# Key reads of a fused perceiver block shared by two DMA queues, input in four loads, narrow tiles copied by ScalarE

## What is computed

```python
x = x + xattn(layernorm(x), ctx, ctx, Wq, bq, Wk, bk, Wv, bv)   # softmax over 1601 keys
x = x + attn(layernorm(x), ...)     # sigmoid((align-0.295)*15) * gate_q * gate_k, 16 heads of 32
h = layernorm(x)
logits = h @ gate_w.T               # 8 experts
sel, rw = argmax(logits), sigmoid(max(logits))
for e in range(8):
    xs = h * (rw * (sel == e))[:, None]
    out += (xs @ w_up[e].T) * silu(xs @ w_gate[e].T) @ w_down[e].T
x = x + out
```

## Time and profile before

| | us |
|---|---|
| runs | 333.71 median (331.84 to 335.01, 3 runs) |
| the profiled execution | 333.99, its span 332.3 |
| TensorE busy | 301.6 (91%) |
| VectorE busy | 161.2 (49%) |
| ScalarE busy | 90.7 (27%) |
| GpSimd busy | 78.4 (24%) |

### The profile page before, as it was taken

How to read it: one execution, slowest core, us unless ns; L and a number is a source line. 1 busy time by engine, 2 the same in 40 slices (tenths; PEclk the granted TensorE clock), 3 DMA queues, 4 the chain that set the end, 5 groups by cost and what they waited for, 6 DMA issues and landing times. The chain is left out here.

```text
span 332.3 us, 5209 instructions
## 1 busy us (share of the span) xinstructions
PE 301.6 (91%) x1806; PEld 159.8 (48%) x1806; DVE 161.2 (49%) x364; ACT 90.7 (27%) x209; POOL 78.4 (24%) x84
## 2 busy tenths in 40 slices
PE   0999899999899889999989999999998989899792
PEld 0788567643454544445455445455543344443330
DVE  3303338537263763828185833738561354735431
ACT  1132230235112346321234442124411013411110
POOL 5000003167022500112340020135102246103202
PEclk9999999999999999999999999999999999999998
DMA  7999999999999998999949699952715996153300
GB/s 250 390 374 172 184 311 387 211 187 257 387 211 228 279 187 132 375 250 227 324 77 192 116 393 220 258 204 83 298 63 145 396 411 266 28 205 109 119 2 34
DMA packets 61364, 74.27 MB, mean 224 GB/s; under 512 B 3187, under 2 KB 40083, under 8 KB 60320
## 3 DMA queue, kind: packets, MB, share of 16 engines
q1 hardware_dynamic: 59792, 69.23, 80.2%
q0 software_dynamic: 1552, 4.78, 4.0%
HBM read 70.85 MB, written 3.67 MB: 224 GB/s over the span
## 5 line engine op out<-in xcount | busy, mean ns | idle before, releaser
L1251 PE MATMUL SC<-CT_sb,QC_sb 128*64 128x256 f32 x384 | 50.4, 389 | 0.3 <-DVE CT_sb L847 0.2
L847 DVE STREAM_TRANSPOSE CT_sb<-FF_sb 128x1024 f32<-128x1024 f32 x36 | 42.4, 1220 | 14.3 <-DMA FF_sb<-ctx 12.7
L1290 PE MATMUL ST<-CTX_sb,PR_sb 128*64 128x512 f32 (+1 forms) x208 | 48.2, 600 | 1.1 <-ACT PR_sb L347 1.1
L1251 PEld LDWEIGHTS SC<-CT_sb,QC_sb 128*64 128x64 f32 x384 | 24.7, 136 | 17.2 <-issue 9.0
L1176 PE MATMUL A<-AW_sb,normT_sb 128*128 128x512 f32 x64 | 29.4, 599 | 1.3 <-DVE normT_sb L918 1.3
L1290 PEld LDWEIGHTS ST<-CTX_sb,PR_sb 128*64 128x64 f32 (+1 forms) x208 | 13.9, 136 | 23.2 <-issue 22.3
L532 POOL TENSOR_TENSOR rn_sb<-ss_sb,nhalf_sb 128x16 f32<-128x16 f32 x4 | 11.7, 2915 | 33.9 <-DVE ss_sb L923 33.9
L1176 PEld LDWEIGHTS A<-AW_sb,normT_sb 128*128 128x128 f32 x64 | 11.7, 190 | 14.8 <-issue 12.2
L1169 PE MATMUL TR<-ident_sb,CTX_sb 128*128 128x128 f32 (+1 forms) x128 | 16.1, 266 | 2.3 <-DVE CT_sb L340 1.1
L1196 PE MATMUL A<-AW_sb,WQK_sb 128*128 128x256 f32 x64 | 16.4, 422 | 0.8 <-ACT AW_sb L645 0.8
L1169 PEld LDWEIGHTS TR<-ident_sb,CTX_sb 128*128 128x128 f32 (+1 forms) x128 | 12.9, 141 | 8.7 <-issue 5.6
(11 more groups left out here) (227 smaller groups left out, 459.0 us busy)
## 6 DMA issues: line engine op xcount, KB each, us to landing
CTX_sb<-ctx SPq DMA_DIRECT2D x24, 1024.0 KB, 10.7
FF_sb<-ctx SPq DMA_DIRECT2D x80, 128.0 KB, 7.2
FF_sb<-ctx SPq DMA_DIRECT2D x32, 256.0 KB, 7.9
CTX_sb<-wgu SPq DMA_DIRECT2D x4, 1024.0 KB, 9.4
CTX_sb<-wdn SPq DMA_DIRECT2D x5, 512.0 KB, 12.8
FF_sb<-wgu SPq DMA_DIRECT2D x2, 1024.0 KB, 6.6
rows<-XR_sb SPq DMA_DIRECT2D x3, 512.0 KB, 10.7
CTX_sb<-ctx SPq DMA_DIRECT2D x8, 130.0 KB
```

The source lines that it names most:

```text
L847: v.transpose(ctxT[:, pos % 2, k, :, :].rearrange("p c (b r) -> p b c r", r=Q), split[:, k, at:at + BLOCKS, :].rearrange("p b (c r) -> p b ...
L1251: last = t_.matmul(out[q, :], (qcurP if split_group else qcur)[:, c, q], ctxT[:, pos % 2, k, c, 0:n], start=(c == 0), stop=(c == DC - 1))
L1290: last = t_.matmul(ST[q, :], probs[0:w, t, q], ctxb[0:w, k, t, :], start=(t == 0), stop=(t == KT - 1))
```

## The change

SP now issues only the reads of quarters 0 and 1 (`LOWER`, partitions 0 to 63); ScalarE issues those of quarters 2 and 3 (`UPPER`, 64 to 127). Groups 4 and 5 become one part of 256 KB reads. For pair 0 ScalarE's reads stand one by one behind its copies of the queries; later they stand in fours (`upper_first`, `upper_rest`). x is loaded in four pieces with a power each, and the loads of `rowv` and `gwT` are issued behind these powers. TensorE does 9 matmuls on the identity while it waits (`START_FILL`). On VectorE, in pair 0, the transpose of group 1 moves behind the last gate sums and the last copy of numerators. ScalarE copies both narrow tiles, and VectorE reads the number of rounds earlier.

```diff
-SPLIT_PARTS = ((1, 2), (3,), (4,), (5,))
+SPLIT_PARTS = ((1, 2), (3,), (4, 5))
+LOWER, UPPER = ([(quad, k) for quad in range(lo, lo + QUADS // 2) for k in range(2)] for lo in (0, QUADS // 2))
+UPPER_REST, UPPER_FIRST = 1, 5
+START_FILL = 9
-XT_BY_ACT = (3, 5)
+XT_BY_ACT = (3, 4, 5)
...
+        def load_split(eng, p, part, quads):
+            first, slot = SPLIT_PARTS[part][0] * GT * P, SLOT_OF[SPLIT_PARTS[part][0]]
+            n = len(SPLIT_PARTS[part]) * BLOCKS
+            for quad, k in quads:
+                src = A["ctx"][bass.ds(2 * p + k, 1), first:first + n * Q, quad * P:(quad + 1) * P]
+                eng.dma_start(split[quad * Q:(quad + 1) * Q, k, slot * BLOCKS:slot * BLOCKS + n, :],
+                              src.rearrange("a (b r) d -> r (a b) d", r=Q)).then_inc(s_split[part], 16)
...
                 sp.wait_ge(s["keysT_made"], split_turned(p, len(order_of(p).split)))
                 settle(sp)
-                load_split(p + 1, 0)
+                load_split(sp, p + 1, 0, LOWER)
...
                 sp.wait_ge(s["keysT_made"], split_turned(p, 2))
                 settle(sp)
-                load_split(p, 2)
-                load_split(p, 3)
+                load_split(sp, p, 2, LOWER)
...
+            for t in range(PAIRS):
+                if t == 2:
+                    load_weight(wq, "wq", "wq_in")
+                sp.dma_start(xall[:, t, :], A["x"][t * P:(t + 1) * P, :]).then_inc(s[f"x_in{t}"], 16)
...
+            for t in range(PAIRS):
+                pool.wait_ge(s["ln0_eps"], t + 1)
+                g.tensor_tensor(rstd[:, t:t + 1], rstd[:, t:t + 1], nhalf[:, 0:1], ALU.pow).then_inc(s["ln0_pow"], 1)
             pool.dma_start(rowv[:], A["rowv"].partition_broadcast(P)).then_inc(s["rowv_in"], 16)
...
+                    if half == 1:
+                        load_split(act, 0, 0, UPPER[m:m + 1])
...
             for m in range(DC):
                 move_qk(True, m)
+                load_split(act, 0, 1, UPPER[m:m + 1])
...
+            def upper_first(p, n, part):
+                act.wait_ge(s["keysT_made"], split_turned(p, n))
+                if not isinstance(p, int):
+                    settle(act)
+                load_split(act, p + 1, part, UPPER)
+
+            def upper_rest(p):
+                act.wait_ge(s["keysT_made"], split_turned(p, 2))
+                settle(act)
+                load_split(act, p, 2, UPPER)
...
             for t in FIRST.tiles[GT:]:
                 move_keys(act, a.copy, 0, 0, t)
+            upper_first(0, 2, 0)
...
                 move_numerators(act, a.copy, 0, c)
+                if c == 0:
+                    upper_first(0, 3, 1)
...
                     move_keys(act, a.copy, p, 0, NEXT.tile(u))
+                    if u == UPPER_REST:
+                        upper_rest(p)
+                    if u == UPPER_FIRST and not is_last(p):
+                        upper_first(p, NEXT.split.index(3) + 1, 1)
                 exponentials(p)
                 for step in by_max:
                     attention(p - 1, step)
                 move_numerators(act, a.copy, p, 0)
+                if not is_last(p):
+                    upper_first(p, len(NEXT.split), 0)
...
             with act.Fori(0, nr) as r:
-                routed(NT - 1, "xT", r)
+                for f in range(NW, NT):
+                    routed(f, "xT", r)
...
             gate_sums(2, 6)
+            move_numerators(dve, v.tensor_copy, 0, 3)
+            gate_sums(6, 2 * DC)
             turn_split(1, NEXT.groups[0])
-            gate_sums(6, 2 * DC)
-            move_numerators(dve, v.tensor_copy, 0, 3)
             turn_split(1, NEXT.groups[1])
...
-                routed(NW, "xT", link, r)
...
+            for _ in range(START_FILL):
+                t_.matmul(AB[0][:, 0:P], ident[:], ident[:], start=True, stop=True)
```

More of the change, by code:

```diff
@@ L359, in load_ctx @@
                     sp.dma_start(ctxb[0:TAIL, k, FULL, :], src).then_inc(s_ctx[k][c], 16)
-            def load_split(p, part):
-                first, slot = SPLIT_PARTS[part][0] * GT * P, SLOT_OF[SPLIT_PARTS[part][0]]
-                n = len(SPLIT_PARTS[part]) * BLOCKS
-                for quad in range(QUADS):
-                    for k in range(2):
-                        src = A["ctx"][bass.ds(2 * p + k, 1), first:first + n * Q, quad * P:(quad + 1) * P]
-                        sp.dma_start(split[quad * Q:(quad + 1) * Q, k, slot * BLOCKS:slot * BLOCKS + n, :],
-                                     src.rearrange("a (b r) d -> r (a b) d", r=Q)).then_inc(s_split[part], 16)
             def next_split(p):
@@ L421, in _ @@
             sp.sem_inc(s["xr_free"], 16)
-            for i in range(2):
-                src = A["x"][2 * i * P:(2 * i + 2) * P, :].rearrange("(a p) d -> p a d", p=P)
-                sp.dma_start(xall[:, 2 * i:2 * i + 2, :], src).then_inc(s[f"x_in{i}"], 16)
-            load_weight(wq, "wq", "wq_in")
+            for t in range(PAIRS):
+                if t == 2:
+                    load_weight(wq, "wq", "wq_in")
+                sp.dma_start(xall[:, t, :], A["x"][t * P:(t + 1) * P, :]).then_inc(s[f"x_in{t}"], 16)
             load_weight(wkT, "wkT", "wkT_in")
@@ L429, in _ @@
                 load_chunk(0, c)
-            load_split(0, 0)
-            load_split(0, 1)
+            load_split(sp, 0, 0, LOWER)
+            load_split(sp, 0, 1, LOWER)
             sp.wait_ge(s["qp_made"], 2 * DC)
@@ L498, in _ @@
                    allow_small_or_imprecise_dtypes=True).then_inc(s["const_made"], 1)
+            for t in range(PAIRS):
+                pool.wait_ge(s["ln0_eps"], t + 1)
+                g.tensor_tensor(rstd[:, t:t + 1], rstd[:, t:t + 1], nhalf[:, 0:1], ALU.pow).then_inc(s["ln0_pow"], 1)
             pool.dma_start(rowv[:], A["rowv"].partition_broadcast(P)).then_inc(s["rowv_in"], 16)
             pool.dma_start(gwT[:], A["gwT"]).then_inc(s["gwT_in"], 16)
-            for i in range(2):
-                pool.wait_ge(s["ln0_eps"], i + 1)
-                g.tensor_tensor(rstd[:, 2 * i:2 * i + 2], rstd[:, 2 * i:2 * i + 2], nhalf[:, 0:2], ALU.pow).then_inc(s["ln0_pow"], 1)
             def pair_queries(p):
@@ L828, in _ @@
             for i in range(2):
-                dve.wait_ge(s[f"x_in{i}"], 16)
                 for t in range(2 * i, 2 * i + 2):
+                    dve.wait_ge(s[f"x_in{t}"], 16)
                     link(v.bn_stats(st[:, t, :], xall[:, t, :]))
                     link(v.bn_aggr(mv[:, t, :], st[:, t, :]))
-                v.tensor_scalar(rstd[:, 2 * i:2 * i + 2], mv[:, 2 * i:2 * i + 2, 1], EPS, None, ALU.add).then_inc(s["ln0_eps"], 1)
-                dve.wait_ge(s["ln0_pow"], i + 1)
+                    v.tensor_scalar(rstd[:, t:t + 1], mv[:, t, 1:2], EPS, None, ALU.add).then_inc(s["ln0_eps"], 1)
                 for t in range(2 * i, 2 * i + 2):
+                    dve.wait_ge(s["ln0_pow"], t + 1)
                     v.tensor_scalar(xn[:, t, :], xall[:, t, :], mv[:, t, 0:1], rstd[:, t:t + 1], ALU.subtract, ALU.mult).then_inc(s["xn_made"], 1)
@@ L1132, in _ @@
             assert n[0] == COUNT_LINKS
-            for f, step in LATE:
-                routed(f, step, link_wide)
+            routed(*LATE[0], link_wide)
             dve.wait_ge(s["rounds_made"], 1)
             nr = dve.value_load(rounds[0:1, 0:1], min_val=1, max_val=MAXR)
+            for f, step in LATE[1:]:
+                routed(f, step, link_wide)
             with dve.Fori(0, nr) as r:
                 link, n = linker("round_chain", COUNT_LINKS + ROUND_LINKS * r)
-                routed(NW, "xT", link, r)
                 link(v.tensor_scalar(tok[:, 0, :], tok[:, 2, :], 0.0, 2.0 * B * S, ALU.is_equal, ALU.mult))
@@ L1451, in routed @@
                     pe.wait_ge(s_got[f], 16 * r + 16)
-                    earlier(pe, "xT_moved", n)
+                    earlier(pe, "xT_moved", n - 1 if f == NT - 1 else n)
                     turn_rows(x_bank(f), got[f], P).then_inc(s["x_turned"], 1)
```

8 lines of the change are left out of this document (4 added, 4 removed).

## The result

The changed kernel takes 347.32 us (344.1 to 350.17), the kernel before 332.92 beside it: a ratio of 1.0393 with an interval of 1.0301 to 1.0485. It is slower by about 4%; forecast were 335.4 and at most 341. Some executions of most kernels here, the one before included, fall into a slower state, so the ratios, and the times of the experiments if nothing else is said, are those of the other runs (in turn_no_start this leaves out two of twelve, of 449 and 775 us) and can differ a little from the quotient of two medians. The profiled execution took 350.17, its span 348.4; the spans of the five other executions are 342.4 to 347.8, so 0.6 to 6 us of the loss that the profile shows are this execution's own.

The account below looks back on a forecast made before the run. TensorE, busy 301.6 of 332.3 us, was the bound, leaving only its start, waits and half-clock matmuls to shorten. 333.99 with -2.4 - 1.5 - 2.0 + 2.1 + 5.2 = +1.4 gave 335.4; own range 332.7 to 338.8, overall 329.5 to 341.

Parts of the forecast that it names:

- Start: Before the first projections: early matmuls raise TensorE's clock sooner, gaining 2.4 us (3.0 at best), which passes through whole.
- End: Narrow tiles: ScalarE copies the first transpose earlier, so the first narrow matmul starts 1.5 us sooner (0.7 if ScalarE pays VectorE's delay).
- Reads in pair 1: Pair 1: fewer SP issues remove TensorE's waits of 0.95 and 1.14 us, gaining 2.0; pairs 2 and 3 gain nothing.
- Rival 4: Group 4 waits for the whole 2 MB part, about 1 us in each of three pairs; 338.9 us, chance 0.10.
- Pair 0 to 1: End of pair 0: gate sums and transposes behind the last copy make ScalarE's scaling and "on" 2.1 us late; bounds 0 to 2.3.
- Boundaries: Pairs 1 to 2 and 2 to 3: part 0's late upper quarters delay "on" 2.6 us each, 5.2 lost; bounds 3.2 to 7.2.
- Rival 2: ScalarE is held at its read issues, 341 us, chance 0.20; sign: issues over 1.2 us and late copies behind them.
- Rivals 1 and 3: Late upper read of part 0 is covered, 330.2 us (chance 0.28); nine matmuls raise the clock too late, 338.0 (0.06).

Follow-up runs that it names:

- turn_no_start: sync_in_turn with the start of the kernel before (two loads of x, powers of two columns, no early matmuls); ratio 0.9943.
- part2_by_sync: The changed kernel, but SyncE issues all eight reads of part 2 (groups 4 and 5) ahead of the chunk reads; 336.9 us, ratio 1.0111.
- chunks_behind: The changed kernel, but SyncE holds its chunk reads behind part 2 until group 4 has been transposed; 338.55 us, ratio 1.0103.
- start_end_order: The kernel before with the change's start, end and VectorE order at the end of pair 0, all reads as before; ratio 1.0003.
- fill_only: The kernel before with the nine early matmuls alone; ratio 0.9997.
- end_only: The kernel before with the change's end alone (ScalarE copies both narrow tiles, first turns ahead of the loop); ratio 0.9943.
- turn_apart: sync_in_turn with groups 4 and 5 as parts of their own again; 330.68 us, ratio 0.9905.
- sync_in_turn: The changed kernel, but SyncE issues all of part 2 and of pairs 2 and 3's part 0, lower and upper quarters alternating; 329.57 us, ratio 0.9905.
- all_by_sync: The changed kernel with every read back on SyncE, parts still merged; 341.26 us, ratio 1.0240.
- parts_apart: The changed kernel with groups 4 and 5 read as two parts again, both still shared by the two queues; 340.57 us, ratio 1.0166.

## Why the prediction was wrong

- **Start, -2.4.** It was -3.26, a little beyond the good end of its bounds, and the clock was up at 8. "It passes through whole, as TensorE has little idle time behind it up to pair 1" came true for this kernel's reads, though not for the reason it gives, which is luck. With the shared first reads the start did pass: group 3 of pair 1 starts at 91.8 in part2_by_sync and chunks_behind and at 93.69 before, which is the start's 2.6 to 2.7 less the 0.7 that B is longer. In the profiled execution of the change 3.1 of it went to the fall of the clock at 52. With the old reads next to nothing of it passed (start_end_order, fill_only), because part 0 of pair 1 came no earlier, or hardly (transposed at 77.16 and 75.14, at 75.66 before); VectorE already waited 1.86 us for it in the kernel before, and the forecast had not looked there.
- **End, -1.5.** Right: -1.53, and -1.41 in end_only.
- **Reads in pair 1, -2.0, "in pairs 2 and 3 nothing".** This step failed, and it is the largest error. Half of the -2.0 came: the wait of 0.95 us for chunk 0 is gone. For the other half and the "nothing" stand +2.93, +3.37 and +2.30 (C, E, G), 9.6 of the 14.7 us by which the span missed the forecast. The reading of the 1.14 us was right, as it is 0.22 in turn_apart, where group 4 is there in time, but its condition "if groups 4 and 5 land in time" did not hold. The forecast asked how many issues SyncE saves, and not what stands beside ScalarE's reads once they are in a queue of their own. In SyncE's one queue part 2 went ahead of the chunks. In two queues, the half that was issued late shared the engines with chunks that were wanted last.
- **Rival 4** had the place (group 4) but not the cause: it priced the merged part at 180 GB/s as 1 us a pair. The merged part alone costs nothing in pair 2 and up to 0.8 in pair 3, and in pair 1 between nothing (part2_by_sync, turn_no_start) and 3 to 4 (sync_in_turn against turn_apart, all_by_sync against start_end_order); what decides that, no run here shows. In pairs 2 and 3 of the change it took the competing queue as well to make it 3.4 and 2.3.
- **Pair 0 to 1, +2.1.** Right, at 1.9: the reduction ahead of the scaling (L894, now L924) starts 5.97 us behind TensorE's last turn of pair 0, and started 4.09 behind it. B as a whole, with the reads' gain in it, is +0.7 (42.58) where the clock stays up and part 0 is there.
- **Boundaries, +5.2.** The mechanism and the wait were right: part 0 was there 9.1 and 7.4 us behind ScalarE's copy, forecast were 8 to 9, and "on" came 3.2 and 2.5 us later, 5.7 in all. Where the clock stayed up (F of part2_by_sync, parts_apart and chunks_behind) the boundary cost 2.5 to 2.8, the forecast's 2.6. The term missed the clock behind a stop: D and F of the change lost 8.5, the rest of it behind the two falls of the clock.
- **Rival 2** is refuted as a cost, though its sign is there once: four issues took ScalarE 1.9 to 3.7 us, one of them alone 2.07, and behind the slowest four an activation (L710) came 0.8 us late (4.89 us idle ahead of it for 4.06 in pair 3), for which TensorE did not wait:

```profile
162.28 3.73 ACTq L359 DMA_DIRECT2D FF_sb<-ctx  x4
166.12 0.69 ACT L710 ACTIVATE vs_sb<-A,ratio_sb 128x512 f32<-128x512 f32 x1 [4.89 <-PE A L1206]
```

- **Rivals 1 and 3** are refuted: the late upper half was not covered (VectorE waited 7.50 and 5.76 us for it), and the clock was up at 8.
- **The range.** Its good end was added up with +2.1 for pair 0 to 1, where the term's own lower bound is 0; with that the sum is 330.6 and not 332.7. It changes nothing here, since the miss is at the other end.
- **Open.** The 3 us at 52 to 59 us fall in some executions of kernels with the early matmuls, with TensorE busy; the four profiled kernels without these matmuls had none there, too few to call it a cause, and no run here tells what decides it. They are in the profiled span, and only in part in the median.

## What to carry over

Within SyncE's queue what was issued first was served first; moving half of a transfer to another queue gives that up, so ask what else will be in flight between its issue and its use, and issue both halves at the same moment or leave it. Where a gain lies ahead of a stretch that waits for reads, it is worth nothing until those reads move too: mark a few fixed points in both traces and subtract, and the lost microseconds show where they go. A stop of about 2 us on TensorE can cost 1 to 2 us more in its clock, and a profile of one execution shows whether it did only for that execution.
